# A graph network of two layers: both layers written out, the second over fixed ranges of nodes

## The reference

```python
neigh_sum = segment_sum(x[src], dst, num_segments=N)
deg = segment_sum(ones, dst, num_segments=N)
neigh_agg = where(deg > 0, neigh_sum / maximum(deg, 1), x)
x = layernorm(x + relu(concat([x, neigh_agg]) @ W.T + b))
Q, K, V = type_matmul(x, W_Q, ntype), type_matmul(x, W_K, ntype), type_matmul(x, W_V, ntype)
k_t = type_matmul(K[src], W_edge, etype)
scores = sum(Q[dst] * k_t, -1) / sqrt(128) * mu[etype]
attn = exp(scores - seg_max[dst]) / (seg_sum[dst] + 1e-10)      # softmax over the edges of one dst
x = layernorm(x + segment_sum(V[src] * attn[:, None], dst, num_segments=N))
```

## Time and profile before

| | us |
|---|---|
| median of 3 runs (lowest, highest) | 3644.12 (3643.68, 3648.20) |
| the profiled execution, device time | 3643.21 |
| its span, first to last instruction | 3641.4 |
| TensorE busy | 2582.1 (71%) |
| VectorE busy | 1966.3 (54%) |
| ScalarE busy | 1669.3 (46%) |
| GpSimd busy | 1643.9 (45%) |
| chain that ended last: GpSimd, TensorE, issue | 42%, 31%, 16% |
| mean of the DMA traffic | 80 GB/s |

### The profile page before, as it was taken

How to read it: one execution, slowest core, us unless ns; L and a number is a source line. 1 busy time by engine, 2 the same in 40 slices (tenths; PEclk the granted TensorE clock), 3 DMA queues, 4 the chain that set the end, 5 groups by cost and what they waited for, 6 DMA issues and landing times.

```text
span 3641.4 us, 65169 instructions
## 1 busy us (share of the span) xinstructions
PE 2582.1 (71%) x17382; PEld 1930.5 (53%) x17382; DVE 1966.3 (54%) x7136; ACT 1669.3 (46%) x3211; POOL 1643.9 (45%) x1680
## 2 busy tenths in 40 slices
PE   1999999999999999945555565655555565655555
PEld 0556565656565656635545454545545454545545
DVE  7766666666666666633444444444444444444444
ACT  3666666666666666612333333333333333333333
POOL 6000000000000000037777777777777777777774
PEclk9999999999999999977777777777777777777777
DMA  9011111111111111133333333333333333333332
GB/s 106 16 42 42 42 42 42 42 42 42 42 42 42 42 42 42 42 102 109 109 110 108 110 108 109 109 108 109 108 110 108 110 108 109 109 108 110 108 110 70
DMA packets 239976, 291.93 MB, mean 80 GB/s; under 512 B 135316, under 2 KB 183381, under 8 KB 233557
## 3 DMA queue, kind: packets, MB, share of 16 engines
q0 software_dynamic: 75440, 205.65, 19.5%
q1 hardware_dynamic: 157881, 81.62, 8.6%
q10 hardware_dynamic: 6508, 3.33, 0.4%
HBM read 229.43 MB, written 61.04 MB: 80 GB/s over the span
## 4 chain that ended last, share of the span: by engine, by line
POOL 42%; PE 31%; issue 16%; DVE 7%; ACT 1%; DVEq 1%; ACTq 1%; POOLq 1%; DMA 0%; SPq 0%
POOL ring L608 41%; PE banks L672 15%; PE banks L665 6%; DVE sums L1173 2%; DVE sums L1172 2%; PE banks L714 1%; PE banks L719 1%; PE banks L723 1%; PE banks L732 1%; PE banks L729 1%; PE banks L682 1%; DVE work L1231 1%; PE banks L707 1%; POOL ring L564 1%; ACT negmax L928 1%
## 5 line engine op out<-in xcount | busy, mean ns | idle before, releaser
L608 POOL DMA_INDIRECT ring<-kv_table,stage x1568 | 1527.9, 974 | 490.7 <-issue 490.7
L672 PE MATMUL banks<-sums,negmax 128*128 128x385 bf16 x4802 | 1095.7, 327 | 0.0
L928 ACT ACTIVATE negmax<-banks 128x392 bf16<-128x392 f32 x1568 | 776.2, 498 | 486.3 <-PE banks L665 480.3
L828 PE MATMUL banks<-identf,ring 128*128 128x128 f32 x1568 | 300.1, 354 | 890.5 <-DMA ring<-kv_table,stage 848.3
L828 PEld LDWEIGHTS banks<-identf,ring 128*128 128x128 f32 x1568 | 238.5, 183 | 927.4 <-issue 870.3
L594 POOL COPY ring<-ring 128x1024 f32<-128x1024 f32 x49 | 57.4, 1172 | 1444.1 <-ACT ring L954 1444.1
L672 PEld LDWEIGHTS banks<-sums,negmax 128*128 128x128 bf16 x4802 | 463.8, 97 | 306.4 <-issue 39.8
L1172 DVE TENSOR_SCALAR sums<-iota_n,keys_g 128x128 bf16<-128x128 bf16 x1568 | 429.3, 274 | 300.8 <-PE banks L665 275.1
L1018 ACT ACTIVATE work<-banks 128x512 f32<-128x512 f32 x392 | 220.5, 586 | 808.2 <-PE banks L828 808.2
L665 PE MATMUL banks<-sums 128*128 128x392 bf16 x1568 | 517.6, 331 | 59.4 <-DVE sums L1173 32.9
L1173 DVE TENSOR_SCALAR sums<-iota_k,keys_g 128x392 bf16<-128x392 bf16 x1568 | 503.8, 321 | 0.0
(11 more groups left out here) (220 smaller groups left out, 2988.0 us busy)
## 6 DMA issues: line engine op xcount, KB each, us to landing
kv_table<-ring SPq DMA_DIRECT2D x49, 1024.0 KB, 4.2
ring<-kv_table,stage POOLq DMA_INDIRECT x1568, 2.8
queries<-queries_t SPq DMA_DIRECT2D x196, 32.0 KB, 1.9
x_rows<-ring SPq DMA_DIRECT2D x49, 64.0 KB, 1.6
queries_t<-q_tile SPq DMA_DIRECT2D x49, 64.0 KB, 4.0
src_idx<-x_rows SPq DMA_DIRECT2D x98, 32.0 KB, 2.5
out_dram<-src_idx SPq DMA_DIRECT2D x97, 32.0 KB, 2.4
ring<-in_x_dram SPq DMA_DIRECT2D x48, 64.0 KB, 3.8
```

The costliest lines, as they stand in the source:

```text
L608: pool.indirect_dma_start(rows[u][:, j, :], None, table_, bass.IndirectOffsetOnAxis(ap=stage[:, u, j:j + 1], axis=0)).then_inc(s, 16)
L672: mm = pe.matmul(bank[2 + par][:, 0:3 * D + 1], picked[:, par, h, :], x_parts[:, h, 0:3 * D + 1], start=(h == 0), stop=(h == TILES - 1))
L828: tr = pe.transpose(bank[g % 2][:, j * P:(j + 1) * P], kv_ring[new.u][:, g * 4 + j, 0:D], identf[:, :])
L928: act.activation(picked[:, par, :, c * NW:(c + 1) * NW], bank[c % 2][:, 0:KEYS].rearrange("p (h w) -> p h w", w=NW), ACT.Copy).then_inc(pi ...
```

## The change

- The loops over passes are gone, both layers are written out for each block with constant waits and constant addresses. Edges outside of the fixed ranges are taken in two separate loops with registers: in layer one column by column over pairs of tiles (`gen_...`), in layer two for tiles of 125 nodes over pairs of columns (`far_...`). The check now only sets their counts. Where all edges are in range, every count is 1, the loops run once with data that match nothing, and one copy from `y_dram` to the output is made.
- Layer two has one fixed range of 128 nodes for each block, from 64b - 32, for all 16 columns. The state (rows and sum of 128 nodes) is one small tile, of which half is finished and reset after each block. A correction is one column instead of a replicated row; the 64-wide windows, their bases, `spread`, `delta`, `factor`, `sums` are gone.
- The mask is four bf16 matmuls with 4 rows: constant 1 and three digits of the edge's destination (square terms and products, so that the sum is 0 at the right node and a large negative number elsewhere). The digits are made on VectorE by nine operations at the head of steps 4 to 12 of layer one, stored to DRAM and loaded for each block by SP.
- Scores are 4 products with 128 query columns (before with 64), probabilities 16 transposes and four copies, all on VectorE; value products have 128 columns.
- Edges are loaded once, in natural columns, and the index for the gathers is made from them; five slots instead of four.

The diff, cut to its core:

```diff
+        def sweep(body):
+            for g in range(3):
+                body(g, None, None)
+            for t in range(TILES - 2):
+                body(2 * t + 3, tile(t), None)
+                body(2 * t + 4, None, tile(t))
+            body(NBLK - 1, tile(TILES - 2), None)
...
+        def far_sweep(e, begin, body, end):
+            e.wait_ge(general_ready, 1)
+            tiles, runs = general(e, 2, FAR_TILES), general(e, 5, FAR_RUNS)
+            with e.Fori(0, tiles) as i:
+                begin(i)
+                with e.Fori(0, runs) as c:
+                    body(i * FAR_RUNS + c, c)
+                end(i)
...
@@ sync @@
-                gate(sp, nat_pads, ps_ * 2 + 3)
-                load_columns(sp, key_i, src, L["nat"])
-                load_columns(sp, rel_nat.bitcast(I32), dst, L["nat"])
+            with sp.Fori(0, copies) as i:
+                sp.dma_start(out[bass.ds(i * COPY, COPY), :], y_dram[bass.ds(i * COPY, COPY), :]).then_inc(out_stored, 16)
...
@@ gpsimd @@
+            pool.tensor_scalar(spare_n[:, :], src_n[:, :], float(ET), None, ALU.mult).then_inc(pool_step, 1)
+            pool.tensor_tensor(et_n[:, :], spare_n[:, :], et_n[:, :], ALU.add).then_inc(pool_step, 1)
+            pool.tensor_copy(key_f, et_n[:, :]).then_inc(keys_nat, 1)
...
-                gate(pool, l1_idx, ps_ * (NBLK + AHEAD) + i * SLOTS1 + u + 1)
-                for h in range(2):
-                    gate(pool, part_ps, ps_ * (2 * NBLK) + i * (2 * SLOTS1) + 2 * u + h + 1)
-                    for j in range(RUN):
-                        gather(kv_ring, table, h * RUN + j, u, l1_rows[2 * u + h])
+            far_sweep(pool, lambda i: None, far, lambda i: None)
+            pool.wait_ge(keys_ready, 4)
+            for b in range(NBLK):
+                if b >= SLOTS1:
+                    pool.wait_ge(values_ps, b - SLOTS1 + 1)
+                for j in range(COLS):
+                    gather(b % SLOTS1, j, key_idx[:, b * COLS + j:b * COLS + j + 1])
...
@@ tensor @@
+            def mask(k):
+                if k.b > 0:
+                    pe.wait_ge(prob_ready, k.b)
+                for q in range(4):
+                    pe.matmul(bank[q], places[:, :], moves[k.par][0:4, q * 512:(q + 1) * 512], start=True, stop=False,
+                              skip_group_check=True)
+            def score(k):
+                for g in range(4):
+                    pe.wait_ge(keysT_ready, k.b * 4 + g + 1)
+                    mm = pe.matmul(bank[g], queries[:, :], keysT[:, g, :], start=False, stop=True, skip_group_check=True)
+            def values(k):
+                pe.wait_ge(prob_copied, k.b * 4 + (4 + 8))
+                for j in range(COLS):
+                    mm = pe.matmul(bank[7][:, 0:D], prob[:, j, :], kv_ring[k.u][:, j, D:2 * D],
+                                   start=(j == 0), stop=(j == COLS - 1))
+            for n in range(-1, NBLK + 1):
+                old, new, older = blk(n), blk(n + 1), blk(n - 1)
+                if old:
+                    score(old)
+                if older:
+                    values(older)
+                if new:
+                    transpose_keys(new)
+                if old:
+                    transpose_prob(old, 1 if new else 0)
+                if new:
+                    wait_moves(new)
+                    mask(new)
...
@@ vector @@
+            def l0(g, early, late):
+                if DIGIT_STEP <= g < DIGIT_STEP + DIGIT_OPS:
+                    digit_op(g - DIGIT_STEP)
+                if g > 0:
+                    join_parts(g - 1, 1 - par)
...
+            def maximum(k):
+                dve.wait_ge(score_ps, k.b + 1)
+                dve.reduce_max(largest[:, :], scores, AX).then_inc(largest_ready, 1)
+            def update(k):
+                dve.scalar_tensor_tensor(state[:, D:D + 1], state[:, D:D + 1], corr[:, at], part_sum[:, at], ALU.mult, ALU.add)
+                dve.wait_ge(values_ps, k.b + 1)
+                dve.scalar_tensor_tensor(state[:, 0:D], state[:, 0:D], corr[:, at], bank[7][:, 0:D], ALU.mult, ALU.add)
```

More of the change, by code:

```diff
@@ L991, in _ @@
             act.sem_inc(v_spread, 1)
-            with act.Fori(0, count) as ps_:
-                def start():
-                    tables(ps_)
-                    for c in range(GCOLS):
-                        take(ps_ * NBLK, 0, c, 0)
-                def end(tile, last):
-                    late_part(tile)
-                    copy_x(last)
-                    copy_mean(last)
-                    deviation(last)
-                    late_part(last)
-                first_sweep(act, ps_, start, l0, end)
@@ L1039, in _ @@
-            with act.Fori(0, count) as ps_:
-                for u in range(AHEAD):
-                    stage_block(u, u)
-                second_sweep(act, ps_, l1)
+            tables()
+            for c in range(GCOLS):
+                take(0, c, 0)
+            sweep(l0)
+            late_part(tile(TILES - 2))
+            last = tile(TILES - 1)
+            copy_x(last)
+            copy_mean(last)
+            deviation(last)
+            late_part(last)
+            for q in range(4):
+                act.wait_ge(keys_ps, q + 1)
+                at = slice(q * 512, min(NAT, (q + 1) * 512))
+                act.activation(key_idx[:, at].bitcast(I32), bank[q][:, 0:at.stop - at.start], ACT.Copy).then_inc(keys_ready, 1)
@@ new lines, in far_end @@
+            def far_end(i):
+                gate(act, far_var, i + 1)
+                act.activation(far_rstd, aggr[:, 1:2], ACT.Sqrt, bias=eps_col[:, 0:1]).then_inc(far_std, 1)
+            far_sweep(act, lambda i: None, far, far_end)
+            for n in range(-1, NBLK + 1):
+                old, new, older = blk(n), blk(n + 1), blk(n - 1)
+                if old:
+                    exponent(old)
+                if new:
+                    copy_keys(new)
+                if older and older.b % 2 == 1:
+                    y_deviation(older.b // 2)
@@ L1262, in l0 @@
                     relu(early)
[L1263 to L1264 removed]
+                if g + 2 < NBLK:
+                    hot(g + 2, par, 1)
                 if early:
                     normalise_x1(early)
[L1268 to L1289 removed]
```

1337 lines of the change are left out of this document (674 added, 663 removed).

## The result

| | before | after |
|---|---|---|
| median (lowest, highest), us | 3643.92 (3643.68, 3648.20) | 3535.38 (3534.80, 3537.84) |
| span of the profiled execution, us | 3641.4 | 3533.0 |

The ratio is 0.9701, with a 95% interval of 0.9684 to 0.9718. The spans differ by 108.4 us, where -61.5 was forecast; 3535 us lies 17 us under the forecast range.

What follows compares the result with a forecast made beforehand. It took TensorE's matmuls to bound layer one and GpSimd's 1568 gather issues layer two. Terms -43 + 11 + 3 + 2.5 - 41 + 6 = -61.5 took 3643.2 to 3582 us; range 3552 to 3625.

Steps and rivals of the forecast that it cites:

- Unrolling layer one: Layer one: straight code, constant waits and a single table remove TensorE's waits at loop heads; -43 us (bounds -44 and 0).
- Digits: Layer one, steps 4 to 12: nine VectorE operations at step heads, nearly all paid; +11 us (bounds 0 and 20).
- Setup: Before layer one's sweep: an added cast and generic column against shorter checks; +3 us (bounds -6 and +9).
- junction: Between the layers: useless loads go, but the serial far iteration precedes the main gathers; +2.5 us (bounds -5 and +15).
- Gathers: Layer two: without VectorE's mask operation, one long gather per block goes; -41 us (bounds -45 and 0).
- Others keep up in layer two: Per block, TensorE needs 13.6 us at 2.4 GHz against 20.0 us of gathers, so GpSimd stays last.
- The end: After the last gather: serial remaining work takes 43 us instead of 36.6; +6 us (bounds -3 and +15).
- (1): Rival, layer two: TensorE becomes the bound and the kernel is slower, 3847 us; 6%.
- (2): Rival, layer two: the 0.30 us before every gather are register work that constants remove, 3112 us; 3%.
- (3): Rival, layer two: new SBUF operations hold the gathers as long as before, 3623 us; 9%.
- (4): Rival, layer one: stops stay because straight code must be fetched too, 3625 us; 7%.
- (5): Rival, general loops: they run many times instead of once, a large multiple of the time; 1%.

Runs made afterwards that it cites:

- e1: Kernel before with layer one's inner loop (23 iterations) written out on TensorE, ScalarE and VectorE; 4293.93 us, kernel before 4359.29.
- e2: e1 with layer one's pass loop also removed on the same three engines, so waits compare with constants; 4310.25 us, kernel before 4359.29.
- e11: Changed kernel without the loops for out-of-range inputs (generic column, far tile), last copy kept; 3508.92 us, kernel before 3646.35.
- e9: Kernel before with VectorE's mask comparison made whole for block 0 only (output wrong); 3604.42 us, kernel before 3646.35.
- e14: Changed kernel without the generic column's loop ahead of layer one, far tile's loop kept; 3865.36 us, kernel before 4406.83.
- e4: Same kernel as e9, run in a set where TensorE sets layer two's pace; 4352.63 us, kernel before 4359.29.
- e10: Kernel before with GpSimd's loops of layer two written out, constant addresses and waits; 3647.75 us, kernel before 3646.35.
- e18: e12 plus an engine cursor reset, and the far loop's semaphore subtraction moved so GpSimd needn't wait for far scores; 3832.10 us, kernel before 4369.65.
- e12: Changed kernel with digit operations moved to every second step, where VectorE waits, and the five last padding gathers left out; 3521.15 us, kernel before 3646.35.
- e6: Changed kernel plus the old mask comparison on VectorE in each block, result unused; 3572.79 us, kernel before 3646.73.
- e15: Changed kernel whose far loop waits for a growing gather count instead of subtracting from the semaphore; 3868.86 us, kernel before 4406.83.
- e13: Changed kernel without the far tile's loop ahead of layer two, generic column kept; 3849.55 us, kernel before 4406.83.

## Why the prediction was wrong

**The bounds: right.** TensorE bound layer one and still does, GpSimd's 1568 issues bound layer two and still do, with 0.30 us ahead of each.

**Unrolling layer one: right direction, mis-sized; the step that failed.** The failed step is "the two waits of the earlier trace rows without the 12.8 us are 44.1 us", with 44 as the bound. The loop heads cost 66.6 us (e1), and constant waits 13.4 more (e2), together 80 where 43 stood. It took two wait rows for all stops of the stage. A third row of 22.4 us, as long as either of them, for the chain that ends in L1231, was left out, and 14 us were in no wait row at all. How much of an iteration's 2.9 us is the branch and how much are two table loads, of which the prediction had seen one, stays open. One view would have given most of it: busy time over the whole sweep, 1401.0 of 1470.6. The step used a stretch of 56 us without loop for the state afterwards, and never asked the same of the looped part.

**Digits: half of the price.** +5.4 for +11. Seven of the nine operations took 1.02 us and two 1.89, a mean of 1.2 and not 1.4; and TensorE waited in 7 steps only, 0.8 us each. The slack of 0.2 us had been read at a single step.

**Setup, junction: right within the bounds** (0 for +3, +1.6 for +2.5). The far iteration was priced at 2.5 + 2.8 + 2 + 2.5 = 9.8 us, fully on the path; 9.7 was measured (e11). That it came so close is partly luck: TensorE's part with its copy took 3.8 us for 2, since ScalarE loads a table of 1.28 us in it, and the rest of the way to the main gathers 1.3 for 2.5. The column costs 3.7 (e11); something else won as much back, and the shorter checks are the likely cause, which no run separates.

**Gathers: right operation, one cost missing.** The comparison alone is worth 40.7 us (e9) of the 41. Without the generic loops the change gains 44.9 us here (e11), so short operations in SBUF took none of the 4 us left for them; 11.2 come back, since the median gather takes 7 ns longer once the column loop has run (e14). No row of the trace of before could show that.

**Others keep up in layer two: right on that chip.** TensorE is busy for 1360.3 of 1970.5 us, 13.9 in a block, where the sum gave 13.6 of 20 at full clock. The granted clock was 0.83, so the sum was too high and the nearness is luck. In the three TensorE-paced sets it wasn't so, for a reason that no row of the trace of before showed.

**The end: +0.1 for +6.** The sum added in line what overlaps: transposes (3.3) and four copies of the probabilities (2.8) take 3.2 us together. From the last finish to the issue of the last copy it is 2.5 us and not 4, from there to the end 2.4 and not 4; no row of before had shown these terms. Transposes at the low clock, scores, exponent, values and finishes took some 2.5 us less in all. Against that, the rows of the last gather reach TensorE 5.0 us after its start and not 2.8.

By size: heads -24, constant waits -13, end -6, digits -6, setup -3, junction -1, gathers +7: together -46 as rounded, for 47 us between forecast and spans. (The sweep of before took 1470.6 us in its own trace and 1468.7 in e4, from which the first two are counted.)

**Rivals.** (1) didn't happen on the chip of the prediction. (2) is refuted by e10. (3) isn't what happened: long gathers are gone and new SBUF operations hold none. (4) is the reverse of what came. (5): each loop ran once, but once costs 24.6 us in all, 11.2 of it by way of the gathers; that is the last sign of being wrong that the prediction named, tens of us for the general iterations.

## What to carry to other kernels

Price a stage's stops by the busy time of its bounding engine over the whole stage, and only then by wait rows, which leave out what falls into modelled ends; and when a loop is to be unrolled, count all table loads in it. An iteration that runs once for the sake of rare inputs is a serial chain of waits on the bounding engine's queue: let no wait of it stand ahead of the main stream (e18), and put small extra work where its engine waits already (e12) rather than at a step's head. A comparison of two SBUF operands of 128x1024 on VectorE beside a stream of gathers costs 0.3 to 0.4 us each time (e6, e9).

## What the runs showed of the hardware that was not expected

The pace of layer two differs from set to set, by about 20% for the kernel before. Each set had a chip of its own, and within a set all runs of the kernel before agree within 0.4%, so the chip is the likely cause; in the five sets no chip was used twice. Of TensorE in e4, layer two, score products of before:

```profile
2511.88 0.59 PE L818 MATMUL banks<-work,queries 128*64 128x512 f32 x1 [1.20 <-issue]
2513.28 0.59 PE L818 MATMUL banks<-work,queries 128*64 128x512 f32 x1 [0.81 <-issue]
2514.66 0.97 PE L818 MATMUL banks<-work,queries 128*64 128x512 f32 x1 [0.80 <-issue]
```

In the trace of before the same products come without a gap:

```profile
2527.49 1.93 PE L818 MATMUL banks<-work,queries 128*64 128x512 f32 x7
```

In e4 0.8 to 1.2 us stand ahead of each of the three, and nothing that the profile shows ends the stop. There were 421 such stops ahead of L818, 394 us in e4. The products take longer as well: between 1620 and 4290 us 8355 of them are busy for 1747 us at a granted clock of 0.66; in before, between 1620 and 3600 us, 8484 are busy for 1127 us at 0.75. Which of clock and stops comes first isn't shown. A block takes 2692 / 98 = 27.5 us there for 20.4, and 23.2 in e15, whose straight code has such stops too (480 ahead of the transposes, 478 us). In layer one of the same runs there are none between the products of the sweep. A late supply of instructions while gathers run would look like this, but no run separated it: open. The Trainium skill (Runtime: NRT & Kernel Launch, section Instruction fetch mechanics) has straight code streamed and its fetch mostly hidden; if the stops are the fetch, e15 speaks against that. So the change is worth 3% where GpSimd sets the pace; the changed kernel itself was not run where TensorE does, but kernels that differ from it by one loop or one instruction came out 12 to 13% under the kernel before.

A loop with one gather of other rows, run once and long before, goes with 7 ns more in the median of 1568 later gathers (e14 against e13 and e15).
